# Moving the stores of the quantized weights from GpSimd's DMA queue to SyncE's, in a fused attention and MLP kernel

## The chip, the cores and the metric

One Trainium2 chip, 8 cores, one launch. Batch element b of 4 is handled by cores 2b and 2b+1, each of which produces 2048 of the 4096 rows of that element; the cores run the same program on other data and exchange nothing. The metric is device time in microseconds (us) of the slowest core. "SP" is SyncE, "POOL" GpSimd, "DVE" VectorE, "ACT" ScalarE, "PE" TensorE.

## The reference, cut to what matters

```python
mod = (silu(c) @ wmod).reshape(B, 6, 1, -1)          # sa, ca, ga, sb, cb, gb
h = layernorm(x) * (1 + ca) + sa
k, q, v = h @ Wk.T, h @ Wq.T, h @ Wv.T               # S = 4096, D = 1024
alpha = softmax(q @ (k @ Wa.T).T)
x = x + ga * (alpha @ (v @ Wb.T))
h = layernorm(x) * (1 + cb) + sb
def fake_quant_weight(w):                            # 8 bits, one scale per tensor
    scale = max(abs(w)) / 127
    return clip(round(w / scale), -128, 127) * scale
h = gelu(h @ fake_quant_weight(W_fc).T + b_fc + 2 * (h @ A_fc.T) @ B_fc.T)        # FF = 4096
x = x + gb * (h @ fake_quant_weight(W_proj).T + b_proj + 2 * (h @ A_proj.T) @ B_proj.T)
```

What matters here is that W_fc (4096 x 1024) and W_proj (1024 x 4096) must be scaled, rounded and scaled back before the second half can use them.

## The kernel before, in words

The program is written by hand as one list of instructions for each of the five engines; the order of the calls to `em` is the order in which an engine issues. A wait is a semaphore and a value, and it holds up everything behind it on its engine. A DMA's wait stands on the engine that issues it.

The stages are `ph1` (modulation rows), `ph3` (weights of the attention folded and transposed), `ph4` (layer norm, keys `ak_fm`, values `u_tm`, queries, which go to DRAM as `q_sc`), `ph5` (attention, and beside it the quantization of both MLP weights), `ph6` (the MLP). The change is in `ph5`.

`ph5` loops over 16 query tiles `ic` of 128 rows. In one iteration SP issues the load of this tile's queries into one of two buffers `q_stg` (L1089); PE computes the scores against the first 2048 keys (L1096) into `pE`, DVE takes the maximum (L1104), ACT the exponential `alphaA` (L1108); then come the first half of the product with the values for the tile before (`_emit_pv`, part 0: 16 transposes of `alphaB` at L1070, matmuls L1194), the scores against the other 2048 keys (L1120), the second half of the product (part 1, L1207), and four calls of `quant_slot`. Last come the 16 transposes of `alphaA` (L1070, evicted at L1078). Then the next iteration begins with its `q_stg` load and L1096.

`quant_slot(k)` works on several of the 64 weight tiles of 128 x 1024 at a time, in this order: for tile k-1 two Sign activations on ACT (L946, L949) and two DVE operations (L960, L965); for tile k-2 the scaling into bf16 on ACT (L978), into one of five buffers `qbf`; for tile k the SP load of tile k+1 into one of two buffers `wst` (L916, which waits for L960), the scaling (L920), two casts to int32 on DVE (L927), two casts back on ACT (L930) and one subtraction on POOL (L936); and for tile k-6 `quant_tile_store`: eight PE transposes (L1005), the eviction on DVE back into `qbf` (L1011), and the store of the tile to DRAM (L1023). Tiles 0 to 31 are W_fc and go to `wfcq_sc` in rows of 2 KB; tiles 32 to 63 are W_proj and go to `wpjq_sc` by the access pattern `(j p) o -> p j o`, in pieces of 128 bf16 numbers.

Every store waits for the eviction L1011 and for the landing of the store before it (`t_ser`), so there is never more than one on its way. All of them count on one semaphore, `d_pc0`, on which L978 waits too. The first store is emitted in slot 6, the third slot of iteration 1. Behind the last iteration stand the last product with the values and slots 64 to 69, with the last six stores (tiles 58 to 63). `ph6` begins on SP with the loads of all of `wpjq_sc` (L1265), which wait for the last store.

Other users of the two queues in `ph5`: SP issues `q_stg` (L1089), `x_st` (L1189, the residual row block) and `wst` (L916). POOL issues the store of the attention's result (L1231).

Of the kernel before, what the change touches and what calls it, by code (L numbers as in the profile page):

```python
# [22 lines left out]
class MK:  # L23
# [10 lines left out]
    def em(self, eng, fn, waits=(), inc=None, inc_n=None):  # L34
        if inc is not None and inc not in self.cnt:
            self.cnt[inc] = 0
        for snm, _v in waits:
            if snm not in self.cnt:
                self.cnt[snm] = 0
        if inc is not None and inc_n is None:  # L40
            inc_n = 16 if inc.startswith("d") else 1
        tok = None
        if inc is not None:
            self.cnt[inc] += inc_n
            tok = self.cnt[inc]
        self.ops[eng].append((fn, tuple((s, v) for (s, v) in waits if v), inc, inc_n))
        return tok
# [948 lines left out]
    def quant_tile_store(self, idx):  # L996
        em, s = self.em, self
        st = self._qstate
        pp = idx % 5
        pT = (s.pT0, s.pT1)[idx % 2]  # L1000
        t_b = st["qb"][pp]
        qq = idx % 2
        t_tr = None
        for j in range(8):
            t_tr = em("tensor", lambda e, j=j, pT=pT, pp=pp: e.transpose(  # L1005
                out=pT[:, j * 128:(j + 1) * 128],
                in_=s.qbf[pp][:, j * 128:(j + 1) * 128], identity=s.idb[:, :]),
                waits=[("s", t_b), self.pTst["free"][qq]],
                inc="t" if j == 7 else None)
        self.pTst["tr"][qq] = t_tr  # L1010
        t_ev = em("vector", lambda e, pT=pT, pp=pp: e.tensor_copy(  # L1011
            out=s.qbf[pp][:], in_=pT[:]),
            waits=[("t", t_tr)], inc="v")
        self.pTst["free"][qq] = ("v", t_ev)
        t_ser = ("d_pc0", self.cnt.get("d_pc0", 0))
        if idx < 32:
            dst = s.wfcq_hbm[idx]
        else:
            k = idx - 32
            dc, pc = k // 4, k % 4  # L1020
            dst = s.wpjq_hbm[pc * 1024:(pc + 1) * 1024, dc * 128:(dc + 1) * 128] \
                .rearrange("(j p) o -> p j o", p=128)
        em("gpsimd", lambda e, dst=dst, pp=pp: e.dma_start(  # L1023
            out=dst, in_=s.qbf[pp][:]),
            waits=[("v", t_ev), t_ser], inc="d_pc0")

# [573 lines left out]
```

How the kernel before makes its waits and increments, by code:

```python
        def run_section(engname, engobj):  # L1495
            for fn, waits, inc, inc_n in self.ops[engname]:
                for sname, v in waits:
                    if last_wait[engname].get(sname, 0) < v:
                        engobj.wait_ge(sem[sname], v)
                        last_wait[engname][sname] = v
                instr = fn(engobj)
                if inc is not None:
                    instr.then_inc(sem[inc], inc_n)
```

## Time and profile before

| | us |
|---|---|
| three timed runs | 3258.85, 3322.7, 3396.4 (median 3322.7) |
| the profiled execution, its own time | 3256.1 |
| its span on the slowest core (core 0) | 3254.4 |
| spans of the other cores | 3233.5 to 3247.0 |
| busy on core 0: PE, DVE, ACT, POOL | 1688.4, 1002.0, 764.8, 433.3 |
| mean granted TensorE clock, cores 0 to 7 | 0.758 to 0.762 |

The page gives times of one execution on the slowest core, from the first instruction. "PEclk" is the granted TensorE clock as a share of full speed. "Idle before <-" is the time an engine stood still ahead of a group, and what released it. "To landing" is the time from a DMA's issue to its semaphore.

### The profile page before, as it was taken

What the parts mean: (1) busy time and instruction counts of PE and PEld (TensorE: products, weight loads), DVE (VectorE), ACT (ScalarE), POOL (GpSimd) and SP (SyncE); (2) the same over time, 40 slices, a digit from 0 to 9 for tenths busy, and PEclk for the clock granted to TensorE, in tenths of its full rate; (3) what the DMA queues carried; (4) which work ended last, traced back from release to release, by engine and by line L of the source; (5) the groups of instructions that cost most, each with busy time, mean ns of one, the idle gap of its engine ahead of it and who ended that gap; (6) DMA issues with size and microseconds to landing.
All of it is one profiled execution on the core that took longest, in us unless ns stands there. A gap on an engine that the chain in (4) does not pass through costs nothing.

```text
span 3254.4 us, 24852 instructions; the slowest of 8 cores (3233.5 to 3254.4 us)
## 1 busy us (share of the span) xinstructions
PE 1688.4 (52%) x7864; PEld 758.7 (23%) x7994; DVE 1002.0 (31%) x1773; ACT 764.8 (23%) x1325; POOL 433.3 (13%) x585
## 2 busy tenths in 40 slices
PE   4520041436665464555444555544425858858588
PEld 1110010112232231222222222222211323323223
DVE  3410343434444443334444333444411020110201
ACT  2310101032222312323333232333313122031220
POOL 0001121213333101111111111122210000000000
PEclk9855575758777687777777777777766979979799
DMA  5500424232222211111111211122242213122130
GB/s 145 166 6 19 134 85 135 74 102 70 67 70 68 78 36 45 49 55 62 69 64 64 72 55 55 55 68 65 71 134 74 72 45 94 42 64 66 46 96 27
DMA packets 92298, 233.40 MB, mean 72 GB/s; under 512 B 25380, under 2 KB 25509, under 8 KB 92152
## 3 DMA queue, kind: packets, MB, share of 16 engines
q1 hardware_dynamic: 65000, 160.33, 16.0%
q0 software_dynamic: 27168, 71.47, 6.6%
q8 instruction: 66, 1.08, 0.1%
q14 instruction: 64, 0.52, 0.1%
HBM read 193.85 MB, written 37.88 MB: 71 GB/s over the span
## 4 chain that ended last, share of the span: by engine, by line
PE 35%; DMA 21%; DVE 14%; issue 11%; ACT 11%; POOL 5%; SPq 1%; DVEq 1%; ACTq 0%; POOLq 0%
PE pO L1432 7%; PE pE L1390 5%; DMA amst<-wpj_in 5%; PE pO L1194 4%; DMA wfcst<-wfcq_sc 4%; PE pE L1096 4%; DMA amst<-wfc_in 3%; POOL qt L936 3%; PE pE L1120 3%; PE pO L1207 3%; ACT h_stage L729 3%; DVE qkf L960 2%; DMA wm<-wmod_in 2%; ACT qkf L930 2%; ACT wst L946 2%
## 5 line engine op out<-in xcount | busy, mean ns | idle before, releaser
L1390 PE MATMUL pE<-h,wfcst 128*128 128x512 bf16 x1000 | 247.0, 388 | 59.3 <-DMA wfcst<-wfcq_sc 41.9
L1432 PE MATMUL pO<-wpj_sb,hid 128*128 128x512 bf16 x1000 | 224.4, 379 | 17.7 <-DVE outb L1448 12.0
L936 POOL TENSOR_TENSOR qt<-qt,qkf 128x1024 f32<-128x1024 f32 x64 | 149.7, 2340 | 485.8 <-ACT qkf L930 481.1
L1070 PE MATMUL pT<-idb,alphaA 128*128 128x128 bf16 x256 | 32.2, 307 | 281.8 <-DVE qbf L1011 275.8
L1005 PE MATMUL pT<-idb,qbf 128*128 128x128 bf16 x512 | 48.7, 260 | 220.6 <-DVE qbf L1011 218.2
L621 DVE TENSOR_REDUCE amx<-amst 128x1 f32<-128x256 f32 x256 | 106.8, 418 | 179.7 <-DMA amst<-wpj_in 99.2
L1194 PE MATMUL pO<-u_tm,alphaT 128*128 128x512 bf16 x496 | 134.7, 433 | 46.7 <-DVE alphaT L1078 44.0
L1405 ACT ACTIVATE hid<-pE,bfc_col 128x512 bf16<-128x512 f32 x128 | 88.0, 687 | 240.5 <-PE pE L1398 240.4
L1096 PE MATMUL pE<-ak_fm,q_stg 128*128 128x512 bf16 x496 | 126.2, 418 | 34.1 <-DMA q_stg<-q_sc 30.7
L742 PE MATMUL pE<-h_stage,wkaT 128*128 128x512 bf16 x496 | 125.0, 416 | 33.7 <-ACT h_stage L729 33.3
L960 DVE SCALAR_TENSOR_TENSOR qkf<-wst,qkf 128x1024 f32<-128x1024 f32 x64 | 78.3, 1223 | 192.8 <-ACT wst L946 192.8
L1390 PEld LDWEIGHTS pE<-h,wfcst 128*128 128x128 bf16 x1024 | 92.3, 98 | 189.0 <-issue 101.7
L618 POOL DMA_DIRECT2D amst<-wfc_in x128 | 68.9, 538 | 462.2 <-DVE amx L626 356.5
L1432 PEld LDWEIGHTS pO<-wpj_sb,hid 128*128 128x128 bf16 x1024 | 97.7, 98 | 137.8 <-issue 24.5
L720 PE MATMUL pT<-idb,xnb 128*128 128x128 bf16 x256 | 32.4, 306 | 176.3 <-DVE xnb L708 176.3
L930 ACT ACTIVATE qkf<-qki 128x512 f32<-128x512 int32 x128 | 80.6, 629 | 180.4 <-DVE qki L927 180.4
L1465 POOL DMA_DIRECT2D out<-outb x16 | 8.6, 538 | 833.3 <-DVE outb L1459 833.3
L760 PE MATMUL pO<-wvbT,h_stage 128*128 128x512 bf16 x504 | 115.6, 379 | 7.0 <-DVE u_tm L772 6.1
L1423 DVE CAST lora1p<-pE 16x512 bf16<-16x512 f32 x4 | 2.7, 679 | 376.7 <-PE pE L1415 376.7
L1120 PE MATMUL pE<-ak_fm,q_stg 128*128 128x512 bf16 x497 | 113.8, 383 | 6.8 <-ACT alphaA L1108 6.0
L1129 DVE TENSOR_REDUCE mcol<-pE 128x1 f32<-128x2048 f32 x16 | 36.7, 2292 | 248.7 <-PE pE L1120 248.7
L1207 PE MATMUL pO<-u_tm,alphaT 128*128 128x512 bf16 x511 | 113.1, 379 | 0.1
(187 smaller groups left out, 2609.4 us busy)
## 6 DMA issues: line engine op xcount, KB each, us to landing
wfcst<-wfcq_sc SPq DMA_DIRECT2D x128, 256.0 KB, 2.6
wm<-wmod_in SPq DMA_DIRECT2D x32, 768.0 KB, 4.5
x_st<-x_in SPq DMA_DIRECT2D x48, 512.0 KB, 3.4
amst<-wfc_in POOLq DMA_DIRECT2D x128, 128.0 KB, 2.7
amst<-wpj_in POOLq DMA_DIRECT2D x128, 128.0 KB, 2.7
wst<-wfc_in SPq DMA_DIRECT2D x32, 512.0 KB, 3.3
wst<-wpj_in SPq DMA_DIRECT2D x32, 512.0 KB, 4.1
x_sc<-x1b POOLq DMA_DIRECT2D x16, 512.0 KB, 3.5
```

The lines of the kernel that those rows point to most:

```text
L621: t_r = em("vector", lambda e, c0=c0, c1=c1, first=first, p=p: e.tensor_reduce(out=s.amx[:, (c0 if first else c1):(c0 if first else c1) + ...
L742: t_mm = em("tensor", lambda e, oc=oc, ic=ic, g=g, sl=sl: e.matmul(out=s.pE[:, sl * 512:(sl + 1) * 512], lhsT=s.wkaT[:, ic * 1024 + oc * 1 ...
L760: t_mm = em("tensor", lambda e, tt=tt, vc=vc, ic=ic, g=g: e.matmul(out=s.pO[:, vc * 512:(vc + 1) * 512], lhsT=s.h_stage[:, ic * 512 + tt * ...
L930: t_kf = em("scalar", lambda e, qkf=qkf, hh=hh: e.activation(out=qkf[:, hh * 512:(hh + 1) * 512], in_=s.qki[:], func=AF.Copy), waits=[("v" ...
L936: t_dd = em("gpsimd", lambda e, qt=qt, qkf=qkf: e.tensor_tensor(out=qt[:], in0=qt[:], in1=qkf[:], op=OP.subtract), waits=[("s", t_kf)], in ...
L960: t_e1 = em("vector", lambda e, qkf=qkf, wsb=wsb: e.scalar_tensor_tensor(out=qkf[:], in0=wsb[:], scalar=0.5, in1=qkf[:], op0=OP.mult, op1= ...
L1096: t_eA = em("tensor", lambda e, oc=oc, jb=jb, p=p: e.matmul(out=s.pE[:, jb * 512:(jb + 1) * 512], lhsT=s.q_stage[p][:, oc * 128:(oc + 1) * ...
L1120: t_eB = em("tensor", lambda e, oc=oc, jb=jb, p=p: e.matmul(out=s.pE[:, jb * 512:(jb + 1) * 512], lhsT=s.q_stage[p][:, oc * 128:(oc + 1) * ...
L1194: em("tensor", lambda e, jc=jc, vc=vc: e.matmul(out=s.pO[:, vc * 512:(vc + 1) * 512], lhsT=s.alphaT[:, jc * 128:(jc + 1) * 128], rhs=s.u_t ...
L1207: t_pv = em("tensor", lambda e, jc=jc, vc=vc: e.matmul(out=s.pO[:, vc * 512:(vc + 1) * 512], lhsT=s.alphaT[:, jc * 128:(jc + 1) * 128], rh ...
L1390: t_mm = em("tensor", lambda e, ic=ic, oc=oc, p=p, sl=sl: e.matmul(out=s.pE[:, sl * 512:(sl + 1) * 512], lhsT=wfcst[p][:, ic * 128:(ic + 1 ...
L1432: t_mm = em("tensor", lambda e, tt=tt, vc=vc, hc=hc: e.matmul(out=s.pO[:, vc * 512:(vc + 1) * 512], lhsT=hid[:, hc * 512 + tt * 128:hc * 5 ...
```

## The change

The store of a quantized tile is issued by SP in place of POOL. Its source, target, waits and semaphore stay as they were.

```diff
@@ quant_tile_store
-        em("gpsimd", lambda e, dst=dst, pp=pp: e.dma_start(
+        em("sync", lambda e, dst=dst, pp=pp: e.dma_start(
             out=dst, in_=s.qbf[pp][:]),
             waits=[("v", t_ev), t_ser], inc="d_pc0")
```

On SP, over one iteration of `ph5` (here a late one, from the residual's load to the next one; `q_stg` is the query tile, `wst` a raw weight tile, `qbf` a quantized tile), the order before is

```order
L1189 DMA x_st0<-x_in 128x1024
L916 DMA wst1<-wpj_in 128x1024
L916 DMA wst0<-wpj_in 128x1024
L916 DMA wst1<-wpj_in 128x1024
L916 DMA wst0<-wpj_in 128x1024
L1089 DMA q_stg1<-q_sc 128x1024
```

and of the changed kernel, in the iteration whose stores pass from W_fc to W_proj,

```order
L1189 DMA x_st0<-x_in 128x1024
L916 DMA wst1<-wpj_in 128x1024
L1023 DMA wfcq_sc<-qbf0 128x1024
L916 DMA wst0<-wpj_in 128x1024
L1023 DMA wfcq_sc<-qbf1 128x1024
L916 DMA wst1<-wpj_in 128x1024
L1023 DMA wpjq_sc<-qbf2 128x8x128
L916 DMA wst0<-wpj_in 128x1024
L1023 DMA wpjq_sc<-qbf3 128x8x128
L1089 DMA q_stg0<-q_sc 128x1024
```

A store now stands behind each weight load, and one stands directly ahead of the `q_stg` load of the next iteration. Its two waits, for the eviction L1011 and for the store before it, stand in SP's list there.

On POOL the slots of one iteration before are

```order
L1231 DMA x1_sc<-x1b 128x1024
L936 TENSOR_TENSOR qt0<-qt0,qkf0 128x1024
L1023 DMA wpjq_sc<-qbf4 128x8x128
L936 TENSOR_TENSOR qt1<-qt1,qkf1 128x1024
L1023 DMA wpjq_sc<-qbf0 128x8x128
L936 TENSOR_TENSOR qt0<-qt0,qkf0 128x1024
L1023 DMA wpjq_sc<-qbf1 128x8x128
L936 TENSOR_TENSOR qt1<-qt1,qkf1 128x1024
L1023 DMA wpjq_sc<-qbf2 128x8x128
L1231 DMA x1_sc<-x1b 128x1024
```

and of the changed kernel

```order
L1231 DMA x1_sc<-x1b 128x1024
L936 TENSOR_TENSOR qt0<-qt0,qkf0 128x1024
L936 TENSOR_TENSOR qt1<-qt1,qkf1 128x1024
L936 TENSOR_TENSOR qt0<-qt0,qkf0 128x1024
L936 TENSOR_TENSOR qt1<-qt1,qkf1 128x1024
L1231 DMA x1_sc<-x1b 128x1024
```

The stores have left POOL, where each had stood behind the subtraction of its slot.

At the end of `ph5` SP's list now holds the last six stores itself, between the last residual load and the MLP's weights:

```order
L1189 DMA x_st0<-x_in 128x1024
L1023 DMA wpjq_sc<-qbf3 128x8x128
L1023 DMA wpjq_sc<-qbf4 128x8x128
L1023 DMA wpjq_sc<-qbf0 128x8x128
L1023 DMA wpjq_sc<-qbf1 128x8x128
L1023 DMA wpjq_sc<-qbf2 128x8x128
L1023 DMA wpjq_sc<-qbf3 128x8x128
L1265 DMA wpj_sb<-wpjq_sc 128x1024 x32
```

Before, the six stood on POOL and SP went from L1189 to L1265. PE's, DVE's and ACT's lists are unchanged.

## Rows read from the trace of the kernel before

**Rows 1.** Windows, `ph5`: us; busy PE, PEld, DVE, ACT, POOL; clock; DMA share
```profile
1228.00:2412.00 1184.00, 577.46 (x3030) 291.60 (x3078) 454.42 (x620) 363.33 (x401) 202.15 (x144) 0.73 0.18 61
```

**Rows 2.** Chain that ended last, end of iteration 4: start us, us, what
```profile
1561.78 1.24 DVE qkf L960
...
1571.39 1.24 DVE qkf L960
...
1576.36 0.70 DVE qbf L1011
1577.06 0.14 issue
1577.19 1.01 PE pT L1070 x8
...
1578.43 7.69 PE pE L1096 x31
```

**Rows 3.** Timeline of POOL, same iteration: start us, us, what [idle before]
```profile
1567.71 2.34 POOL L936 TENSOR_TENSOR qt<-qt,qkf 128x1024 f32<-128x1024 f32 x1 [6.78 <-ACT qkf L930]
1570.00 0.55 POOL L1023 DMA_DIRECT2D wfcq_sc<-qbf  x1
```

**Rows 4.** All 64 stores: ns min/median/max, first and last start
```profile
L1023 POOL DMA_DIRECT2D wfcq_sc<-qbf x32: 549/552/571, 1355.5 to 1918.9; - x32
L1023 POOL DMA_DIRECT2D wpjq_sc<-qbf x32: 887/896/934, 1928.5 to 2409.2; - x32
```

**Rows 5.** Timeline of SP, end of the same iteration
```profile
1572.69 0.33 SPq L916 DMA_DIRECT2D wst<-wfc_in  x1
1573.11 0.39 SPq L1089 DMA_DIRECT2D q_stg<-q_sc  x1
```

**Rows 6.** Chain, from the end of iteration 0 into iteration 1
```profile
1287.14 1.24 DVE qkf L960
...
1288.43 0.33 SPq L916
...
1288.81 3.63 DMA q_stg<-q_sc
1292.44 0.63 issue
1293.07 8.71 PE pE L1096 x31
```

**Rows 7.** DMA issues: KB each, median us from issue to landing
```profile
wfcq_sc<-qbf POOLq DMA_DIRECT2D x32, 256.0 KB, 2.3
wpjq_sc<-qbf POOLq DMA_DIRECT2D x32, 256.0 KB, 2.8
```

**Rows 8.** Landing times of the 16 `q_stg` loads of core 2
```profile
DMA to landing us min/median/max: 2.5/4.6/5.6
```

**Rows 9.** The `wpj_sb` loads on SP: ns min/median/max
```profile
L1265 SPq DMA_DIRECT2D wpj_sb<-wpjq_sc x32: 326/521/1189, 2412.4 to 2430.8; - x32
```

**Rows 10.** DMA, 2392 to 2412: POOL's queue, packets, MB, share of 16 engines
```profile
q0 software_dynamic: 480, 1.57, 20.7%
```

**Rows 11.** PE: L1194 of iteration 1, L1096 of iteration 2, L1194 of iteration 5
```profile
1305.51 7.07 PE L1194 MATMUL pO<-u_tm,alphaT 128*128 128x512 bf16 x31 [2.85 <-DVE alphaT L1078]
...
1363.96 9.10 PE L1096 MATMUL pE<-ak_fm,q_stg 128*128 128x512 bf16 x31 [0.22 <-issue]
...
1590.64 7.97 PE pO L1194 x29
```

**Rows 12.** Windows, start of L1096 in iteration 5; columns as in rows 1
```profile
1577.00:1580.00 3.00, 2.58 (x12) 1.57 (x14) 1.34 (x3) 0.17 (x1) 2.69 (x2) 0.50 0.20 81
```

**Rows 13.** Chain, end of `ph5`: first and last of the six last stores
```profile
2392.08 2.85 DMA wpjq_sc<-qbf
...
2409.20 2.91 DMA wpjq_sc<-qbf
...
2412.43 0.33 SPq L1265
```

## The prediction

> **What bounds the kernel now.** I first read the page's chain of waits and then the windows by stage, and only the attention stage `ph5` matters: it takes 1184 us, and no engine is busy for half of it [rows 1]. It is bound by latency, a chain that passes from engine to engine. Then I read the chain itself over one iteration. The loop has two kinds of links. In the first half PE leads: scores, product, scores, product. In the second half come four quantization slots of 9.61 us each (from 1561.78 to 1571.39, L960 to L960) [rows 2]. The last slot ends with the DVE eviction L1011 at 1577.06; PE transposes `alphaA` from 1577.19, and the next iteration's first matmul L1096 starts at 1578.43 [rows 2]. From L1096 of iteration 2 (1363.96 [rows 11]) to that of iteration 5 (1578.43) are three iterations, 71.5 us each.
>
> The question is whether a store of a quantized tile is in this chain today. On POOL it is not: the subtraction L936 waited 6.78 us for ACT, and the store is issued at 1570.00, behind it, in a gap where POOL has nothing else to do [rows 3]. So POOL gives up 32 x 0.55 + 32 x 0.90 = 46 us of busy time [rows 4], and all of it lies in idle time.
>
> **The change, part by part.**
>
> *POOL.* Removed: 64 issues, worth 46 us of POOL and, by the reading above, 0 us of the span. Its cover is the 6.8 us gap per slot; the chance that it is not covered is a rival below. The store itself also goes out about 2.5 us earlier, right behind its eviction and not behind the subtraction. That makes `d_pc0` earlier for L978, which is not in the chain of a slot.
>
> *SP inside an iteration.* Today SP issues the slot's weight load when L960 ends and then waits for nothing until the next slot. The new store waits for L1011, some 4.4 us later in the slot (1577.06 against 1572.63), and SP is needed again only at the next slot's L960, 5 us after that. So the first three stores of an iteration delay no weight load: cost 0, covered by these 5 us. The wait for the previous store is covered too: it was issued 9.6 us earlier and lands within 3 us [rows 7].
>
> *SP at the seam of two iterations.* This is the place that counts. Behind the fourth slot's weight load stands, today, the `q_stg` load at 1573.11 [rows 5], early enough that PE waits for nothing at 1578.43. In the changed order the fourth store stands between them, and it waits for the eviction that ends at 1577.06 [rows 2]. What is queued behind it is the `q_stg` load, and who waits for that is PE's L1096, the head of the chain. Step by step for a W_fc store: SP wakes 0.05 us after DVE (L960 ends at 1288.38, SP issues at 1288.43 [rows 6]), so the store is issued at 1577.11; with 0.33 us for a plain issue and 0.05 between two, the `q_stg` load is issued at 1577.5, 4.4 us later than before. From issue to PE's first matmul I take the only place in the trace where PE did wait for this load: issue at 1288.81, matmul at 1293.07, 4.26 us (3.63 to landing, 0.63 after it), with a DMA of 512 KB issued 0.38 us ahead of it [rows 6]. So L1096 starts at 1581.8 in place of 1578.43: **+3.3 us**. Lower end: the quickest landing of this load is 2.5 us [rows 8], plus 0.63: start at 1580.6, +2.2. Nothing excludes that end, since the store ahead is 256 KB and not 512. No end lies below zero: even the quickest lands behind 1578.43.
>
> For a W_proj store, in pieces of 128 numbers, SP's issue and the landing behind it are not in the trace. On POOL the same pieces cost 0.34 us more of issue and 0.5 us more to landing [rows 4, 7]. I take the landing difference, which holds the issue, and round it with what the next load may lose behind it to 0.9: **+4.2 us**. Lower end: as cheap as a W_fc store with a landing of 3.0, +2.7. Upper end: the slowest SP issue, 1.19 us [rows 9], and the slowest landing, 5.6 us [rows 8]: load issued at 1578.35, matmul at 1584.6, +6.2. For W_fc the same worst landing gives +5.3; I use 4.2 as its upper end, since 14 loads will not all be the slowest of 16.
>
> How often: the stores begin in slot 6, so the loads for tiles 2 to 15 have a store ahead of them, 14 in all. The store ahead of tile ic's load is weight tile 4 ic - 7, which is a W_proj tile (32 or more) from ic = 10. So 8 x 3.3 + 6 x 4.2 = 26.4 + 25.2 = **+52 us**. Nothing after it absorbs the delay: the rest of an iteration waits for PE's scores. Ends: 8 x 2.2 + 6 x 2.7 = 34, and 8 x 4.2 + 6 x 6.2 = 71.
>
> A place to weigh a rule: the store and the load now share SP's queue. The row says that POOL's six last stores kept the 16 DMA engines busy for 20.7% of 20 us, 0.69 us for each [rows 10]. The Trainium skill ("DMA: Bandwidth & Descriptors", section "Queues, rings and completion order") says that descriptors of one such queue are consumed in ring order on each DMA engine, so the load's data would stand behind the store's. The same page's section "Bandwidth" says why small descriptors to DRAM are slow. By these rules the seam would be nearer the upper end for W_proj; if queues did not matter, the load would land as if alone, near the lower end. No row of before has the two in one queue.
>
> *TensorE's clock.* At the start of L1096 the granted clock is 0.50 of full speed, the 1.2 GHz level [rows 12], after slots with little PE work. A later start changes where in L1096 and L1194 the clock rises. Iteration 1, where PE also stood still ahead of L1096, took 8.71 us for L1096 and 7.07 for L1194 [rows 6, 11], 15.8 together; iteration 5 took 7.69 and 7.97 [rows 2, 11], 15.7 together without its first two matmuls. The slowest L1096, 9.10 [rows 11], with the slower L1194 would be 17.1, 1.4 more. I take 0, with ends of -0.5 and +1.4 per iteration, that is -7 and +20 over 14.
>
> *The end of `ph5`.* Before, the six last stores run one after the other from 2392.08 to SP's first MLP load at 2412.43, 3.39 us each [rows 13], of which up to 0.9 is POOL's issue [rows 4]. On SP each is issue plus landing; as a plain SP issue is 0.33, it may be 0.6 us shorter, or with slow small pieces as much longer. I take 0, ends -4 and +4. SP's residual load for the last tile is now behind a store as well, some 15 us before it is needed: 0.
>
> *Sum.* 3256 (the profiled execution's own time; its span is 3254.4) + 52 + 0 + 0 = **3308**. The three timed runs are 3258.85, 3322.7 and 3396.4: the profile stands with the lowest of them, 2% under the median, and shows nothing of where the other two spend more. I keep to the profile and let the range reach up for a set of runs whose middle one lies higher.
>
> **The rivals.**
>
> *Slow small stores and a worse clock.* The same seam, with every term at its bad end: 3256 + 71 + 20 + 4 = 3351; halfway there it is 3330. For it: no row shows small pieces on SP's queue, and core 2's loads landed in up to 5.6 us. Against it: 8 of the 14 stores are in 2 KB rows. It is slower by over 2% from +65 us, that is from 4.6 us per seam.
>
> *POOL was in the chain after all.* The mechanism that goes the other way: if each issue on POOL held the subtraction of its slot, or what it feeds, 46 us would go. With the seam at its lower end the time would be 3256 - 46 + 34 = 3244, and without a cost at the seam 3210. Up to 1.4% faster, and over 2% only if the slots gained more than the issues themselves. It would decide if the next subtraction ever started right behind a store. Against it: the 6.78 us of idle ahead of it, until ACT. The Trainium skill speaks for this rival: "SBUF — State Buffer" warns that descriptors of GpSimd's DMAs are held up while DVE works in its fast modes. The 32 issues of a kind lie within 549 to 571 and 887 to 934 ns [rows 4], so the trace does not bear it out, and the chance stays small.
>
> *The seam is hidden.* The order may be as shown and PE still not wait, if the load landed 1.5 us after issue: 3256. For it: a load alone is quicker than the median 4.6. Against it: no landing is under 2.5 us [rows 8], and 0.63 follows.
>
> **How the numbers follow.** This kernel's measurement can tell about 2% (65 us) from no change. The forecast, 3285 to 3321, has 0.62; the slower rival, beyond 3321, 0.28; the hidden seam 0.06; POOL in the chain 0.04, of which 0.02 for over 2% faster. Hence faster 0.02, within 2% 0.70, slower 0.28. The range goes from 3275, a little above the sum of the low ends (3256 + 34 - 7 - 4 = 3279) with room for the trace's own error, to 3375: the high end is 3351, and it is raised by 24 for runs whose median is above the profile.
>
> **What would show it.** Right: on SP's queue the `q_stg` load issued about 0.4 us behind a store; in PE's waits "L1096 <- DMA q_stg" about 14 times with 2 to 5 us each where there was one; a period of 75 us for W_fc and 76 for W_proj; slots still 9.6 us; POOL 46 us less busy. Wrong: slots shorter than 9.6 us (POOL mattered), L1096 with no idle before it (hidden), or a period that grows by more than the wait (the clock).

## The result, and the profile after

The changed kernel takes 3299.1 us (median of 10 runs, 3287.1 to 3373.5); the kernel before takes 3258.2 in 10 runs (3252.2 to 3396.4). The ratio is 1.012, with a 95% interval of 1.0095 to 1.0144: slower by about 40 us, under the 2% that were taken as the bound, but clear of noise. In some runs of either kernel the cores of one die or of both are granted a lower TensorE clock and the run takes some per cent longer; the ratios are of the other runs.

With ten runs the median of before fell from 3322.7, over three runs, to 3258.2, close to its profiled execution (3256.1).

The page of the changed kernel is that of core 1. Its heading, the packets, and the groups that answer to the ones of interest, with their columns (busy us, mean ns of one | idle time ahead in us, what ended it):

```profile
span 3298.8 us, 24981 instructions; the slowest of 8 cores (3272.5 to 3298.8 us)
...
DMA packets 125067, 233.41 MB, mean 71 GB/s; under 512 B 58148, under 2 KB 58277, under 8 KB 124920
...
L936 POOL TENSOR_TENSOR qt<-qt,qkf 128x1024 f32<-128x1024 f32 x64 | 149.7, 2339 | 515.3 <-ACT qkf L930 515.3
L1096 PE MATMUL pE<-ak_fm,q_stg 128*128 128x512 bf16 x512 | 148.2, 461 | 82.2 <-DMA q_stg<-q_sc 82.2
```

PE's idle time ahead of L1096 is now 82.2 us and all of it ends with the `q_stg` load. Before, on core 0, the only wait for it was that of iteration 1, 30.7 us. POOL's busy time on the page went from 433.3 to 389.0 us; its idle time ahead of L936, still for ACT, grew from 485.8 us to 515.3.

Cores 0 to 3 of this profile ran their PE at a lower clock in iterations 1 and 2 (on core 1 the L1120 of iteration 1 took 8.58 us at a granted clock of 0.81, where it took 7.07 at 1.00 before), which the runs below with the same seams do not repeat. On these cores the two iterations together grew by 17 to 20 us, on cores 4 to 7 by 5 to 7. So I read core 7 from here on. Its span is 3233.5 before and 3272.5 after, 39 us more.

The end of an iteration in the changed kernel, core 7, by the chain of waits (start, us, what), answers to [rows 2, 5 and 6]:

```profile
1573.23 0.70 DVE qbf L1011
...
1574.06 0.33 SPq L1023
...
1574.47 2.71 DMA q_stg<-q_sc
1577.19 0.25 issue
1577.43 4.61 PE pE L1096 x13
```

This is the seam (the place where one iteration meets the next) as the prediction drew it: eviction, store on SP 0.13 us after its end, load 0.41 us behind the store, matmul. From issue to matmul are 2.96 us, against the 4.26 taken from iteration 1 [rows 6].

The timelines of L1096 on core 7, in iterations 1, 9 and 15, before:

```profile
1281.41 8.79 PE L1096 MATMUL pE<-ak_fm,q_stg 128*128 128x512 bf16 x30 [30.27 <-DMA q_stg<-q_sc]
1854.40 9.45 PE L1096 MATMUL pE<-ak_fm,q_stg 128*128 128x512 bf16 x32 [0.25 <-DMA q_stg<-q_sc]
2283.84 8.10 PE L1096 MATMUL pE<-ak_fm,q_stg 128*128 128x512 bf16 x32
```

and after:

```profile
1279.66 9.11 PE L1096 MATMUL pE<-ak_fm,q_stg 128*128 128x512 bf16 x32 [30.41 <-DMA q_stg<-q_sc]
1878.00 8.62 PE L1096 MATMUL pE<-ak_fm,q_stg 128*128 128x512 bf16 x32 [2.67 <-DMA q_stg<-q_sc]
2328.65 8.57 PE L1096 MATMUL pE<-ak_fm,q_stg 128*128 128x512 bf16 x32 [2.93 <-DMA q_stg<-q_sc]
```

Iterations 1 to 9 hold the eight seams with a W_fc store. They took 572.99 us and now take 598.34: +25.4, or 3.2 per seam. Iterations 9 to 15 hold the six with a W_proj store: 429.44 and 450.65, +21.2, or 3.5 per seam. Together +46.6.

The end of `ph5` on core 7 gives a little back. The first and the last of the six last stores and SP's next issue, in the chain; before:

```profile
2381.09 2.87 DMA wpjq_sc<-qbf
...
2398.28 2.85 DMA wpjq_sc<-qbf
2401.45 0.33 SPq L1265
```

and after:

```profile
2423.15 3.81 DMA wpjq_sc<-qbf
2427.03 2.34 DMA wpjq_sc<-qbf
...
2436.76 2.40 DMA wpjq_sc<-qbf
2439.49 0.33 SPq L1265
```

20.4 us before, 16.3 now: -4.0. There is a second gain ahead of these stores. The last product with the values, L1194 behind the last iteration, took 9.81 us before and 7.07 now. Its rows, and one stretch inside each with its granted clock (the third number from the end, 0.50 and 1.00); before:

```profile
2358.83 9.81 PE L1194 MATMUL pO<-u_tm,alphaT 128*128 128x512 bf16 x32 [0.94 <-DVE alphaT L1078]
2361.00:2364.00 3.00, 3.00 (x9) 1.04 (x8) 0.00 (x0) 0.42 (x1) 0.00 (x0) 0.50 0.00 0
```

and after:

```profile
2404.12 7.07 PE L1194 MATMUL pO<-u_tm,alphaT 128*128 128x512 bf16 x32 [0.94 <-DVE alphaT L1078]
2406.00:2409.00 3.00, 3.00 (x16) 1.37 (x14) 0.00 (x0) 0.20 (x1) 0.00 (x0) 1.00 0.00 0
```

That is -2.7 us, given back by the clock: before, the engine began this product at the 1.2 GHz level and rose in the middle of it; now it ran at 2.4 GHz throughout. Six of the eight cores of the changed kernel show it. From the last L1096 to SP's first L1265 core 7 took 117.6 us before and 110.8 now, 6.8 less. So 46.6 - 6.8 = 39.8 of the loop and its end stand against 39 in the span. This core also reached iteration 0 1.8 us earlier in the second execution, so about 1 us is left for the MLP.

### The profile page after: what moved, and what is told of

The parts are those of the page before. It is cut to its first block, busy times and chain, and to the rows that moved or that the text cites. A ratio compares the mean times of both kernels' runs of the same rounds, so it can differ in the third digit from the quotient of the medians.

```text
span 3298.8 us, 24981 instructions; the slowest of 8 cores (3272.5 to 3298.8 us)
## 1 busy us (share of the span) xinstructions
PE 1704.9 (52%) x7994; PEld 757.2 (23%) x7994; DVE 1001.0 (30%) x1773; ACT 762.5 (23%) x1325; POOL 389.0 (12%) x521
## 2 busy tenths in 40 slices
DMA packets 125067, 233.41 MB, mean 71 GB/s; under 512 B 58148, under 2 KB 58277, under 8 KB 124920
## 4 chain that ended last, share of the span: by engine, by line
PE 34%; DMA 23%; DVE 14%; issue 11%; ACT 10%; POOL 5%; SPq 1%; DVEq 1%; ACTq 0%; POOLq 0%
PE pO L1432 7%; DMA amst<-wpj_in 5%; PE pE L1390 5%; PE pE L1096 4%; DMA wfcst<-wfcq_sc 4%; PE pO L1194 4%; PE pE L1120 3%; POOL qt L936 3%; DMA amst<-wfc_in 3%; PE pO L1207 3%; DVE qkf L960 2%; ACT h_stage L729 2%; DMA wm<-wmod_in 2%; ACT qkf L930 2%; DMA q_stg<-q_sc 2%
## 5 line engine op out<-in xcount | busy, mean ns | idle before, releaser
L936 POOL TENSOR_TENSOR qt<-qt,qkf 128x1024 f32<-128x1024 f32 x64 | 149.7, 2339 | 515.3 <-ACT qkf L930 515.3
L1096 PE MATMUL pE<-ak_fm,q_stg 128*128 128x512 bf16 x512 | 148.2, 461 | 82.2 <-DMA q_stg<-q_sc 82.2
L1194 PE MATMUL pO<-u_tm,alphaT 128*128 128x512 bf16 x512 | 126.6, 411 | 43.3 <-DVE alphaT L1078 43.3
L1120 PE MATMUL pE<-ak_fm,q_stg 128*128 128x512 bf16 x512 | 117.6, 390 | 6.0 <-ACT alphaA L1108 6.0
```

Source lines behind the costliest of these rows:

```text
L936: t_dd = em("gpsimd", lambda e, qt=qt, qkf=qkf: e.tensor_tensor(out=qt[:], in0=qt[:], in1=qkf[:], op=OP.subtract), waits=[("s", t_kf)], in ...
L1096: t_eA = em("tensor", lambda e, oc=oc, jb=jb, p=p: e.matmul(out=s.pE[:, jb * 512:(jb + 1) * 512], lhsT=s.q_stage[p][:, oc * 128:(oc + 1) * ...
L1120: t_eB = em("tensor", lambda e, oc=oc, jb=jb, p=p: e.matmul(out=s.pE[:, jb * 512:(jb + 1) * 512], lhsT=s.q_stage[p][:, oc * 128:(oc + 1) * ...
L1194: em("tensor", lambda e, jc=jc, vc=vc: e.matmul(out=s.pO[:, vc * 512:(vc + 1) * 512], lhsT=s.alphaT[:, jc * 128:(jc + 1) * 128], rhs=s.u_t ...
```

## The experiments

All are made from the kernel before or the changed one, and compared with runs of the kernel before made beside them. Where a kernel uses both queues, it has a second semaphore, `d_pc1`, for SP's stores, and every wait for `d_pc0` is also made for `d_pc1`; its line numbers are up to 4 higher.

**All stores on SP, the query tile loaded early.** Undoes the seam and keeps everything else of the change; the load at the head of the loop stays for iteration 0 alone (cut to the new place of the load).

```diff
             if ic > 0:
                 self._emit_pv(ic - 1, st, emit_trans, part=0)
+            if ic + 1 < NQT:
+                load_q(ic + 1)        # the same dma_start as L1089, with its waits
             t_eB = None
```

> The changed kernel (all 64 stores on SP), but the query tile of iteration ic+1 is loaded right behind the residual load of iteration ic, ahead of the four slots, so no store stands ahead of it. Seam theory: the waits 'L1096 <- DMA q_stg' (14 of 2.3 to 5 us in the changed kernel) go to 0, also the one of iteration 1 (about 4 us of it), and the six last stores keep their 2.4 us each. Ratio to the kernel before 0.997 to 0.999 (-3 to -10 us). Rival, sharing SP's queue costs by itself (stores and weight loads in one queue, slower slots): the slots grow above 9.61 us and the ratio stays at 1.005 to 1.012.

Measured: 0.9958 (0.9939 to 0.9978), faster than before and by more than expected. SP's queue on core 7, end of iteration 4, and L1101, which is this kernel's L1096:

```profile
1563.18 0.33 SPq L916 DMA_DIRECT2D wst<-wfc_in  x1
1567.68 0.33 SPq L1023 DMA_DIRECT2D wfcq_sc<-qbf  x1
1568.05 0.42 SPq L1196 DMA_DIRECT2D x_st<-x_in  x1
1568.57 0.39 SPq L1089 DMA_DIRECT2D q_stg<-q_sc  x1
```
```profile
1567.69 1.01 PE L1070 MATMUL pT<-idb,alphaA 128*128 128x128 bf16 x8 [8.59 <-DVE qbf L1011]
1568.49 6.83 PE L1101 MATMUL pE<-ak_fm,q_stg 128*128 128x512 bf16 x26
```

The store is still issued right behind its eviction, and the `q_stg` load behind it at 1568.57 is now the one for the next iteration: L1101 starts 0.80 us after the last eight transposes do, with no idle time ahead of it. In PE's waits for `q_stg` nothing is left. The slots still take 9.6 us; sharing SP's queue between stores and loads did not make them slower, so that rival is out.

**The kernel before, with only the query load early.** The same edit on POOL's stores.

> The kernel before (stores on POOL) with only the query load moved ahead of the slots. Seam theory: the load was early enough already except in iteration 1, so about -4 us there, ratio 0.997 to 1.000. If the ratio were 0.99 or less, the place of the query load would matter for something other than the stores, and e1 would have to be read against this kernel and not against before.

Measured: 0.9975 (0.996 to 0.999), inside my range. Iteration 1 had waited for its load, and that wait went; it was worth more than the 4 us I gave it. From the L1096 of iteration 0 to that of iteration 2 core 7 took 132.6 us before and takes 125.7 here, 6.9 less. The stores on SP are worth the rest between this kernel and the one above (0.9958 to 0.9975, about 5 us, intervals overlapping), which agrees with the end of `ph5`.

**All but every fourth store on SP.**

```diff
-        em("gpsimd", lambda e, dst=dst, pp=pp: e.dma_start(
+        sp = (idx + 6) % 4 != 3
+        em("sync" if sp else "gpsimd", lambda e, dst=dst, pp=pp: e.dma_start(
```

> Of the stores only those of the fourth slot of an iteration stay on POOL; the other three quarters (and five of the last six) are issued by SP, with a semaphore for each queue. No store stands directly ahead of a query load. Seam theory: no wait of L1096 beyond iteration 1, ratio 0.998 to 1.001. Rival 'relief of POOL is worth something': 35 us of issues leave POOL, ratio 0.99. Rival 'each store on SP costs': 1.006 to 1.010.

Measured: 1.000 (0.9959 to 1.0041). On core 7 the idle time of POOL:

```profile
L936 POOL TENSOR_TENSOR qt<-qt,qkf 128x1024 f32<-128x1024 f32 x64 | 149.7, 2339 | 514.9 <-ACT qkf L930 514.9
```

POOL was relieved of 48 stores, and its idle time ahead of L936 is 514.9 where core 7 had 486.6 before: most of what POOL saved became idle time. The interval alone, 13 us to either side, would not exclude a small relief or a small cost; the loop does it better. From the L1096 of iteration 1 to that of iteration 15 core 7 took 1002.4 us before and 1002.3 here, and no core grew by more than 4 us. So neither 35 us of relief nor a cost of more than about 0.1 us for each store is there.

**Only every fourth store on SP.** The complement, `sp = (idx + 6) % 4 == 3 and idx < 58`.

> The complement: only the stores of the fourth slots (14 of 64) are on SP, the six last ones stay on POOL. Seam theory: the whole loss is here, 14 waits of 3 us and a period longer by 3.3 us: +46 us in the loop and nothing gained at the end, ratio 1.012 to 1.016, at or above that of the changed kernel (1.012). Rival 'each store on SP costs the same': a quarter of it, 1.003.

Measured: 1.0135 (1.0118 to 1.0153). 14 of 64 stores carry the whole loss, and the middle of the interval lies a little above the changed kernel's, as expected if the six last stores gain nothing here. L1096 (here L1099) on core 7, iteration 5:

```profile
1591.36 8.98 PE L1099 MATMUL pE<-ak_fm,q_stg 128*128 128x512 bf16 x32 [2.16 <-DMA q_stg<-q_sc]
```

**The wait without the store.** The kernel before, stores on POOL, but the query load waits for the eviction:

```diff
                 out=s.q_stage[p][:], in_=s.q_hbm[ic]),
-                waits=[("t", st["qs_mm"][p])] + qbar, inc="d_q%d" % p)
+                waits=[("t", st["qs_mm"][p]),
+                       ("v", getattr(self, "t_last_ev", 0))] + qbar,
+                inc="d_q%d" % p)
```

> The kernel before, all stores on POOL, but the query load also waits for the eviction of the last stored tile (the wait that the store ahead of it brings in the changed kernel), so the wait alone is added and no transfer stands ahead of the load. If the wait is nearly all of the loss: 14 waits of L1096 of 2.2 to 2.6 us, the loop 35 to 42 us longer, ratio 1.009 to 1.013. If the transfer of the store ahead of the load in SP's queue is most of it: waits under 1 us, ratio 1.002 to 1.004.

Measured: 1.0092 (1.0077 to 1.0107), 30 us. The chain on core 7, iteration 5:

```profile
1578.06 0.69 DVE qbf L1011
...
1578.83 2.74 DMA q_stg<-q_sc
1581.57 0.25 issue
1581.82 1.44 PE pE L1099 x3
```

The load is issued 0.08 us behind the end of the eviction and lands in 2.74. Core 7's 14 waits average 2.1 us, a little under my bound of 2.2. Against the kernel with only the fourth stores (1.0135, 44 us, or 3.1 per seam), the wait alone is 2.1 per seam, 7 parts in 10. The rest, 1.0 per seam, comes with the store. Of this 0.46 us is its place on SP: the load is issued 0.54 us behind the end of the eviction in the changed kernel and 0.08 here. What is left, about 0.5 us on average (over all cores the waits average 2.1 us here and 3.1 with the fourth stores on SP), is a later landing: the median of a core's 16 `q_stg` loads is 2.6 to 2.9 us here, and 2.9 or 3.0 with the fourth stores on SP, 4.0 on one core. Whether that is the order in SP's queue or only two transfers on the same 16 DMA engines at one time was not tested; it would take a store issued at the same moment from another queue.

**Only W_fc on SP**, `sp = idx < 32`.

> Only the 32 stores of W_fc (rows of 2 KB) on SP: 8 seams. From the trace of the changed kernel (2.4 to 3.5 us of wait by core) 8 x 3.1 = +25 us, nothing at the end of ph5, ratio 1.007 to 1.009.

Measured: 1.0084 (1.0064 to 1.0104), as expected.

**Only W_proj on SP**, `sp = idx >= 32`.

> Only the 32 stores of W_proj (pieces of 128 numbers) on SP: 6 seams and the six last stores. If small pieces cost 0.9 us more at a seam, as the prediction had it: 6 x 4.2 - 4 = +21 us, ratio 1.006. If they cost about 0.4: 6 x 3.6 - 5 = +17 us, ratio 1.005.

Measured: 1.0033 (1.001 to 1.0055), below both figures; 1.005 lies in the interval and 1.006 just above it. The chain on core 7 at one seam:

```profile
2083.89 0.38 SPq L1025
...
2084.36 3.04 DMA q_stg<-q_sc
...
2087.65 8.49 PE pE L1099 x32
```

The store in small pieces costs 0.38 us on SP, 0.05 more than one in rows, and the load behind it lands in 3.04 us where the W_fc seam above had 2.71. The six seams cost 3.1 to 3.3 us each, under the 3.6 (cores 2, 4 and 6: 449.1 to 449.2 us from iteration 9 to 15, where the same cores took 429.3 to 430.6 before). The end gave back 6 to 8 us on these cores where 5 was put in: on seven of the eight cores the last product ran at the high clock here too, which neither figure held.

**Only the six last stores on SP**, `sp = idx >= 58`.

> Only the six last stores on SP. The trace of the changed kernel has them at 2.40 us each where POOL took 3.39, the first one longer (4.2 on the slowest core): the stretch from the first of them to L1265 is 16 to 17 us in place of 20.3, ratio 0.998 to 1.000 (not to be told from 1 by the times, so read in the chain).

Measured: 0.9982 (0.997 to 0.9995). In the chain of core 3, first store, last store, SP's next issue:

```profile
2376.07 2.36 DMA wpjq_sc<-qbf
...
2388.11 2.34 DMA wpjq_sc<-qbf
2390.77 0.33 SPq L1268
```

14.7 us on this core in place of 20.4; the eight cores take 14.7 to 17.6, where they took 20.3 to 21.6 before. This is the part of the gain at the end that the stores themselves bring. The last product took 9.4 us or more on every core here, where it had taken 9.2 or more before. The pattern holds over all the profiles: where the last `q_stg` load was not held up by an eviction (before and five of the experiments) none of 48 cores ran the last product at the high clock from its start, and where it was held up (the changed kernel and three experiments) 24 of 32 did. So the late start of the last iteration goes with this gain. Why the clock then rises earlier stays open: in the 3.1 us ahead of the product core 7's PE ran the same 19 matmuls in both kernels, at a granted clock of 0.50 before and 0.61 after.

The parts add up: the gains and losses of 1.0084 and 1.0033 make 1.0117, and so do those of 1.0135 and 0.9982; the changed kernel has 1.012.

## Why the prediction was right or wrong

**The sum and its base: the step that failed.** The sum added +52 us to the profiled execution and gave 3308. The times in front of it were headed by a median of 3322.7, and against that 3308 says 15 us faster, while the working says slower; the kernel became slower by 41. The step is "I keep to the profile and let the range reach up": two of the three runs lay 2% and 4% above the profile, and the text noted it without deciding which of them the change would be held against. What the runs showed: the profile was the right base (3258.2 over ten runs), and the measured 3299.1 lies 9 us under the forecast and in the range. The change should have been stated as a ratio beside the sum, 1.016, where 1.012 was measured. The low end of the range, 3275, is called a little above 3279 and is a little below it.

**The terms of the sum: 12 us too many.** The prediction had +52; loop and end measured on core 7 make 39.8. The W_fc seams account for 1 us of the difference, the W_proj seams for 4, and the end of `ph5`, put at 0, for 6.8. Each follows below.

**What bounds the stage: right.** A chain of latencies in which POOL's stores have no part; 48 stores taken off POOL gave a ratio of 1.000.

**SP inside an iteration, cost 0: right.** The first three stores of an iteration delay no weight load, by the run with all but every fourth store on SP, and the slots stayed at 9.6 us (SP's weight loads on core 7 of the changed kernel start at 1540.74, 1550.36, 1559.96 and 1569.56).

**The seam for W_fc, +3.3: right in place, and in size by luck, since two errors cancel.** Measured 3.2 per seam. The delay of the load was as drawn, but from its issue to the matmul I took 4.26 us from iteration 1, where a 512 KB load stood ahead; with a 256 KB store ahead it was 2.96. What made up for it: the load's wait is not all of the longer iteration. On core 7 the waits average 2.7 us of the 3.3 that an iteration grew. PE's L1096 and L1194 together took 0.5 us more (16.78 to 17.31, averages over 14 iterations), which I had put at 0 for the clock. At the start of L1096 on core 7 of the changed kernel the granted clock was again at the 1.2 GHz level, as in [rows 12]:

```profile
1577.00:1580.00 3.00, 2.57 (x7) 0.93 (x8) 0.00 (x0) 0.00 (x0) 0.00 (x0) 0.50 0.32 128
```

How much the clock takes at a seam varies by core: on core 4 of the same execution the two took 16.80 before and 16.81 after, so nothing. No experiment isolated it.

**The seam for W_proj, +4.2: mis-sized.** Measured 3.5. The term of 0.9 for small pieces was read from POOL's issue (0.90 against 0.55 us) and landing (2.8 against 2.3). On SP the issue differs by 0.05 us, and what is left is about 0.3 in the landing of the load behind it. Six times 0.7 is 4 us of the miss, the largest error in the loop. This is the mis-sized term: 0.9 us more than at a W_fc seam was forecast, 0.3 was measured.

**The end of `ph5`, 0 with ends of -4 and +4: wrong.** Measured -6.8 on core 7, outside these ends. -4.0 is the stores, whose share the run with these stores alone shows too (0.9982). I had the reason ("it may be 0.6 us shorter") and balanced it with a fear of small pieces that no row supported. The other -2.7 is the clock in the last product. The prediction let the clock shift in the 14 iterations only and never asked what a later start does behind them.

**The rules that were weighed.** On ring order: with the wait alone the load landed in 2.74 us at one seam and with a W_fc store ahead in 2.71 at another, so the transfer ahead of it did not hold it there; with a W_proj store it was 3.04. Over all seams the load did land later with a store ahead, by the 0.5 us above. The wait and the issue account for 2.6 of the 3.1 us at a seam, and ring order for 0.5 at most. On small descriptors being slow: on SP the W_proj stores go out in small packets and keep the DMA engines busy longer (below), and they still landed sooner than on POOL, 2.4 against 2.9 us. On POOL's descriptors being held up by DVE: POOL in the chain had a chance of 0.04, and the run that relieved POOL of 48 stores gained nothing by it.

**The rivals.** The slower one, which began at 4.6 us per seam, had 0.28. On the slowest core of the profile, core 1, the loop grew by 62.4 us, 4.5 per iteration, with waits of 3.6 on average; but 20 us of it lie in the two iterations at the low clock, its W_proj seams cost 3.8 us each, and the run with only the fourth stores on SP shows 3.1 to 3.4 per iteration on its cores. So slow small stores, which this rival rested on, are not there. The hidden seam is excluded by 14 waits.

## What to carry to other kernels

Before a DMA is moved to another engine's queue, list what stands behind it there and when each of those used to be issued. A queue that is almost always idle still has an order (before, SP issued DMAs for some 2 us of a 71.5 us iteration), and here 14 of 64 moved stores, each waiting for something late, cost 44 us because a prefetch stood behind them. If the move is wanted, move the prefetch first: with the query load ahead of the slots the same change gave 0.9958, where the early load alone gave 0.9975. When a forecast is written, the change in time belongs beside the total, with the base named that it is a change of.

## What the runs showed of the hardware

The same stores are cut differently by the two queues. The page of before counts 25380 packets under 512 B, that of after 58148: 32768 more, which is 32 stores of 1024 pieces of 256 bytes. So SP's queue sent each piece as a packet of its own, and POOL's had not: its six last stores went out in 480 packets [rows 10], SP's six in 6240. This is SP's queue on core 7 from 2423 to 2439, columns as in [rows 10]:

```profile
q1 hardware_dynamic: 6240, 1.57, 43.5%
```

The small packets did cost the DMA engines time: 43.5% of 16 us is 1.16 us for each store, where POOL's took 0.69 [rows 10]. In spite of that a store was done sooner from SP, on core 7:

```profile
L1023 SPq DMA_DIRECT2D wpjq_sc<-qbf x32: 359/377/383, 1939.7 to 2436.8; - x32
...
wpjq_sc<-qbf SPq DMA_DIRECT2D x32, 256.0 KB, 2.4
```

The issue takes 377 ns where POOL took 895, and the landing is 2.4 us from issue where it was 2.9; issued one behind the other, that is about 2.4 us per store in place of 3.4, the first of them aside, which took 3.81.
